# Blank padding rows of a sorted token buffer: written over whole regions in an early stage, or per expert right behind the routing

## The reference

```python
scores = softmax(x @ gate_w.T + gate_b)
dispatch = top-2 scores on their experts, 0 elsewhere
for i in range(E):                      # a later expert overwrites an earlier one
    wi = dispatch[:, i:i+1]
    h = relu((x_flat * wi) @ w1[i].T + b1[i])
    y = h @ w2[i].T + b2[i]
    out = where(wi > 0, y, out)
```

## Time and profile before

| | us |
|---|---|
| median of 3 runs | 1758.62 (1758.52 to 1768.12) |
| the profiled execution | 1758.52 |
| its span | 1756.7 |
| PE, DVE, ACT, POOL busy | 1543.0, 1314.9, 1269.7, 520.7 |

### The profile page before, as it was taken

How to read it: one execution, slowest core, us unless ns; L and a number is a source line. 1 busy time by engine, 2 the same in 40 slices (tenths; PEclk the granted TensorE clock), 3 DMA queues, 4 the chain that set the end, 5 groups by cost and what they waited for, 6 DMA issues and landing times. The chain is left out here.

```text
span 1756.7 us, 39269 instructions
## 1 busy us (share of the span) xinstructions
PE 1543.0 (88%) x13958; PEld 838.3 (48%) x13958; DVE 1314.9 (75%) x1924; ACT 1269.7 (72%) x2451; POOL 520.7 (30%) x741
## 2 busy tenths in 40 slices
PE   5999999999988999999999999988999855374297
PEld 4555555555543344343434434436777522123286
DVE  2777777777758999999999999936555438865475
ACT  2777777777753999899989998977888668403186
POOL 0222222222244110101110012117898504223466
PEclk8999999999995999999999999999999966686599
DMA  2121123232204010011001101005443200003120
GB/s 74 29 90 54 54 72 123 72 123 72 86 22 127 11 31 13 5 23 31 4 9 31 28 4 38 5 4 98 97 83 80 47 0 0 0 0 138 53 69 32
DMA packets 49386, 84.80 MB, mean 48 GB/s; under 512 B 19232, under 2 KB 25128, under 8 KB 48752
## 3 DMA queue, kind: packets, MB, share of 16 engines
q1 hardware_dynamic: 43888, 76.25, 16.4%
q0 software_dynamic: 5376, 6.96, 1.5%
HBM read 32.78 MB, written 23.92 MB: 32 GB/s over the span
## 5 line engine op out<-in xcount | busy, mean ns | idle before, releaser
L1049 ACT ACTIVATE m_probs<-m_ring 128x512 f32<-128x512 f32 x1024 | 542.8, 598 | 81.1 <-PE m_ring L965 65.5
L1128 DVE TENSOR_REDUCE m_half_max<-m_pairs 128x2 f32<-128x1024 f32 x512 | 588.1, 1212 | 14.6 <-PE m_pairs L948 14.2
L435 DVE TENSOR_REDUCE a_neg_max<-a_scores 128x1 f32<-128x1024 f32 x257 | 310.5, 1215 | 91.7 <-PE a_scores L362 91.6
L423 ACT ACTIVATE a_probs<-a_scores,a_neg_max 128x1024 f32<-128x1024 f32 x256 | 285.1, 1114 | 124.6 <-DVE a_neg_max L435 124.6
L980 PE MATMUL m_acc<-m_probs,m_v_aug 128*32 128x256 f32 (+1 forms) x4032 | 329.0, 399 | 0.0
L965 PE MATMUL m_ring<-m_q_max,m_k 32*128 32x512 f32 x1024 | 319.3, 501 | 3.9 <-DVE m_q_max L1142 3.0
L948 PE MATMUL m_pairs<-m_k,m_q 32*128 32x512 f32 x1024 | 265.2, 515 | 13.5 <-DVE m_half_max L1128 9.9
L362 PE MATMUL a_scores<-a_q,a_k_own 64*128 64x512 f32 x516 | 261.2, 623 | 6.5 <-ACT a_probs L423 5.6
L362 PE MATMUL a_scores<-a_q,a_k_other 64*128 64x512 f32 x516 | 259.5, 623 | 0.5
L965 PEld LDWEIGHTS m_ring<-m_q_max,m_k 32*128 32x128 f32 x1024 | 146.7, 184 | 219.0 <-ACT m_probs L1049 115.7
L471 POOL TENSOR_TENSOR a_scaled<-values,a_inv 128x128 f32<-128x128 f32 x256 | 102.0, 399 | 366.7 <-DVE a_inv L453 235.7
(11 more groups left out here) (279 smaller groups left out, 2087.0 us busy)
## 6 DMA issues: line engine op xcount, KB each, us to landing
sorted_tokens<-a_blank SPq DMA_DIRECT2D x8, 2176.0 KB
e_gates<-sorted_results SPq DMA_DIRECT2D x64, 256.0 KB, 8.5
a_k_other<-a_k_own SPq DMA_DIRECT2D x66, 128.0 KB, 2.3
m_k<-m_k_init SPq DMA_DIRECT2D x8, 512.0 KB, 7.0
m_q<-xT SPq DMA_DIRECT2D x8, 512.0 KB, 7.6
f_records<-sorted_tokens SPq DMA_DIRECT2D x40, 68.0 KB, 1.8
e_w<-e_w_dram SPq DMA_DIRECT2D x1, 2064.0 KB, 8.0
xT<-x_t_dram SPq DMA_DIRECT2D x1, 2048.0 KB, 7.7
```

Source lines behind the costliest of these rows:

```text
L423: nc.scalar.activation(probs[:, g, :], scores[:, slot(h * G + g), :], ACT.Exp, bias=neg_max[:, g:g + 1], accum_out=total[:, g:g + 1]).then ...
L435: nc.vector.tensor_reduce(neg_max[:, i % G:i % G + 1], scores[:, slot(i), :], AX, ALU.max, negate=True).then_inc(max_done, 1)
L1049: nc.scalar.activation(probs[:, u % SLOTS, head, :], ring[:, bank, :], ACT.Exp, scale=0.5).then_inc(ring_taken, 1)
L1128: nc.vector.tensor_reduce(half_max[:, pair // PAIRS % 2, at:at + 2], pairs[:, pair % 2, :, :], AX, ALU.max).then_inc(pair_taken, 1)
```

## The change

The blank records are no longer written in the first attention. There `blank`, its three semaphores, POOL's memset, `rows_of`, `fill` and the wait for `filled` are taken out, and the input `blank_rows` goes.

In the place stage there is a new tile `blank`, [128, 16, 136]. POOL sets it to zero at the start, waits for `order` and casts 16 columns of it (the `order` array grows by as many) into the row numbers. SP then waits for `blank_set`, behind its loads, and writes the 8 tiles at the end of `scratch` in one DMA (1024 records, 544 KB). DVE, when the last batch is placed, copies the 8 first free rows of the experts to `pad_at` and tells SP (`pads_known`). SP loads each into a register and writes 128 blank records there (68 KB), eight times. Only then does it go on to the table; and it waits for all nine writes (`padded_done`) beside the wait for the scatters.

```diff
@@ -222,8 +210,7 @@
 
-def first_attention_stage(core, xT, y, w_q, w_k, values, loads, scratch, blank_rows):
+def first_attention_stage(core, xT, y, w_q, w_k, values, loads):
 
@@ -263,10 +250,6 @@
         loaded = core.sem("a_loaded")
-        blank = core.sb("a_blank", [D, BLANK_ROWS, RECORD], F32, st)
-        blank_zero = core.sem("a_blank_zero")
-        blank_rows_in = core.sem("a_blank_rows_in")
-        filled = core.sem("a_filled")
         CREDIT = G
@@ -289,29 +272,6 @@
-                def rows_of(e):
-                    sp.wait_ge(blank_zero, 1)
-                    if e:
-                        sp.wait_ge(filled, 32 * e)
-                    sp.dma_start(blank[:, :, D:].bitcast(U32), blank_rows[:, e, :, :]).then_inc(blank_rows_in, 16)
-                def fill(e):
-                    sp.wait_ge(blank_rows_in, 16 * (e + 1))
-                    all_rows = blank[:, :, :].rearrange("p j d -> p (j d)")
-                    at = e * REGION
-                    if e == E:
-                        at += (SORT_TILES - UNUSED) * TILE
-                        sp.dma_start(scratch[at:at + UNUSED * TILE, :].rearrange("(p j) d -> p (j d)", j=BLANK_ROWS),
-                                     all_rows).then_inc(filled, 16)
-                        return
-                    wide = [D, N // (D * BLANK_ROWS), BLANK_ROWS * RECORD]
-                    sp.dma_start(scratch[at:at + N, :].rearrange("(c p j) d -> p c (j d)", p=D, j=BLANK_ROWS),
-                                 all_rows.unsqueeze(1).broadcast_to(wide)).then_inc(filled, 16)
-                    sp.dma_start(scratch[at + N:at + REGION, :].rearrange("(p j) d -> p (j d)", j=BLANK_ROWS),
-                                 all_rows[0:TILE // BLANK_ROWS, :]).then_inc(filled, 16)
 
@@ -319,14 +279,6 @@
                         sp.dma_start(to, at).then_inc(loaded, 16)
-                    else:
-                        e, at = divmod(head - len(loads), 2)
-                        if e <= E:
-                            if at == 0:
-                                rows_of(e)
-                            else:
-                                fill(e)
-                sp.wait_ge(filled, 16 * (2 * E + 1))
                 sp.wait_ge(keys_doubled, DUP * (TILES + 1))
@@ -457,7 +409,6 @@
             def _(pool):
-                nc.gpsimd.memset(blank[:, :, :], 0.0).then_inc(blank_zero, 1)
                 pool.wait_ge(zeroed, 1)
@@ -1878,9 +1829,18 @@
 
+SORT_TILES = (N + E * (TILE - 1)) // TILE + 1
+SORT_TILES += -SORT_TILES % 4
+TABLE = SORT_TILES + 2
 PER = BANK // D
 
+REGION = N + TILE
+UNUSED = 8
+RECORD = D + 8
+DUMP = E + UNUSED
+U32 = mybir.dt.uint32
+I32 = mybir.dt.int32
 
@@ -1902,8 +1862,8 @@
     at = D + E * (PER_BATCH + 1)
-    tile_rows, rows_of_out = order[:, at:at + TABLE], order[:, at + TABLE:at + TABLE + TILES]
-    at += TABLE + TILES
+    tile_rows, rows_of_out = order[:, at:at + TABLE], order[:, at + TABLE:at + TABLE + TILES + DUMP]
+    at += TABLE + TILES + DUMP
     region, earlier_first = order[:, at:at + E], order[:, at + E:at + 2 * E]
@@ -1912,6 +1872,8 @@
         eps = core.sb("p_eps", [D, 1], F32, st)
+        blank = core.sb("p_blank", [TILE, DUMP, RECORD], F32, st)
+        pad_at = core.sb("p_pad_at", [1, E], I32, st)
         turned = core.ps("p_turned", [TILE, 2, BANKS, BANK], st)
@@ -1953,7 +1915,11 @@
         recorded = core.sem("p_recorded")
+        blank_zero = core.sem("p_blank_zero")
+        blank_set = core.sem("p_blank_set")
+        pads_known = core.sem("p_pads_known")
         table_made = core.sem("p_table_made")
+        padded_done = core.sem("p_padded_done")
         scattered = core.sem("p_scattered")
@@ -1978,9 +1944,18 @@
                     sp.dma_start(to, at).then_inc(loaded, 16)
+                sp.wait_ge(blank_set, 1)
+                last = E * REGION + (SORT_TILES - UNUSED) * TILE
+                sp.dma_start(scratch[last:last + UNUSED * TILE, :].rearrange("(t p) d -> p t d", p=TILE),
+                             blank[:, E:, :]).then_inc(padded_done, 16)
+                sp.wait_ge(pads_known, 1)
+                for e in range(E):
+                    at = sp.value_load(pad_at[0:1, e:e + 1], min_val=0, max_val=E * REGION)
+                    sp.dma_start(scratch[ds(at, TILE), :], blank[:, e, :]).then_inc(padded_done, 16)
                 sp.wait_ge(table_made, 1)
                          for t in range(PER)]
+                sp.wait_ge(padded_done, 16 * (E + 1))
                 sp.wait_ge(scattered, 16 * TILES)
@@ -2137,6 +2112,8 @@
 
+                    then(nc.vector.tensor_copy(pad_at[0:1, :], start[0:1, :]))
+                    dve.sem_inc(pads_known, 1)
                     tt(count[:, :], start[:, :], region, ALU.subtract)
@@ -2163,7 +2140,7 @@
                 dve.wait_ge(order_in, 16)
-                nc.vector.tensor_copy(records[:, :, D + 1].bitcast(U32), rows_of_out).then_inc(recorded, 1)
+                nc.vector.tensor_copy(records[:, :, D + 1].bitcast(U32), rows_of_out[:, 0:TILES]).then_inc(recorded, 1)
                 then(nc.vector.tensor_copy(counts[:, :, 0], region))
@@ -2174,6 +2151,10 @@
             def _(pool):
+                nc.gpsimd.memset(blank[:, :, :], 0.0).then_inc(blank_zero, 1)
+                pool.wait_ge(blank_zero, 1)
+                pool.wait_ge(order_in, 16)
+                nc.gpsimd.tensor_copy(blank[:, :, D + 1].bitcast(U32), rows_of_out[:, TILES:]).then_inc(blank_set, 1)
                 for b in range(B):
@@ -2482,7 +2463,7 @@
                     constants.append((tiles.q[0][:, g, :].bitcast(F32), xT[:, PAD + N:PAD + N + S]))
-                first_attention_stage(core, xT, y, w_q, w_k, values, constants, scratch, a["blank_rows"])
+                first_attention_stage(core, xT, y, w_q, w_k, values, constants)
             tiles.add(core, st)
@@ -2602,15 +2583,9 @@
         np.broadcast_to(np.arange(TABLE) * TILE, (D, TABLE)),
-        row[:, None] + TILE * np.arange(TILES),
+        row[:, None] + TILE * np.arange(TILES + DUMP),
         np.broadcast_to(np.arange(E) * REGION, (D, E)),
-    behind_end = N + (row[:, None] * BLANK_ROWS + np.arange(BLANK_ROWS))
-    blank_rows = np.zeros((D, E + 1, BLANK_ROWS, RECORD - D), np.uint32)
-    for e in range(E):
-        blank_rows[:, e, :, 1] = N + TILE * e + (behind_end - N) % TILE
-    blank_rows[:, E, :, 1] = behind_end + TILE * E
 
@@ -2629,7 +2604,6 @@
         "s_w": np.ascontiguousarray(s_w.transpose(2, 0, 1)),
-        "blank_rows": blank_rows,
         "s_vecs": np.ascontiguousarray(s_vecs),
```

More of the change, by code:

```diff
@@ L25 @@
 E = 8
-SORT_TILES = (N + E * (TILE - 1)) // TILE + 1
-SORT_TILES += -SORT_TILES % 4
-TABLE = SORT_TILES + 2
-REGION = N + TILE
-UNUSED = 8
-RECORD = D + 8
-DUMP = E + UNUSED
-BLANK_ROWS = 8
-U32 = mybir.dt.uint32
-I32 = mybir.dt.int32
 class Core:
```

## The result

| | before | after |
|---|---|---|
| median us | 1760.0 (1756.97 to 1770.54, 20 runs) | 1772.05 (1762.65 to 1781.8, 20 runs) |
| ratio, 95% interval | | 1.0058 (1.0040 to 1.0078) |
| span of the profiled execution | 1756.7 | 1781.0 |

The change costs 12 us of the medians, by the interval 7 to 14 us. The profiled execution of after took 1783.15 us, above every other run of it, so its span isn't to be read whole. I followed the same DVE instructions through both traces: the distance after minus before moves by -1.0 us up to the first heads, then by +4.2 in the second attention, +6.3 and +6.0 around 1160 to 1235 us, +8.1 in the place stage and +0.7 behind it: 24.3 us.

What follows compares the result with a forecast made beforehand. POOL's scatters were taken as the path of the place stage. Profiled 1758.52 us + 0 + 0.5 + 0 + 0 + 0 = 1759.0, 1759.1 against the median, stated as 1759; range 1753 to 1766.

Steps and rivals of the forecast that it cites:

- 1. First attention: First attention: removing the small loads, fills and POOL's memset gains 0, at most 0.3 us.
- 2. Start of the place stage: Place stage start: POOL's memset runs beside DVE's first instructions and costs 0.5 us, range 0 to 2.0.
- 3. and 4.: Place stage: the tail write of 544 KB and DVE's extra copy ahead of the table each cost 0.
- 5.: Place stage, SP: eight register loads and pad writes at 1.16 us each end before the scatters land; cost 0.
- SP's pad chain becomes the path: Place stage: SP's pads, dearer beside scatters, outlast them; +4.5 us by issue, +6.6 by landing; chance 0.11.
- The rival of the stall: Place stage: DVE's third-batch stall goes (-5.55 us) or moves, a second in the fourth batch giving +6.3; chance 0.16.
- Fills cost something: First attention: the removed fills had cost time, so the kernel gains 0.3 us, giving 1758.8; chance 0.04.

Runs made afterwards that it cites:

- both: The kernel before, its first-attention fills kept, with the change's whole new part of the place stage added; ratio 1.0055 (1.0035 to 1.0075).
- the second profile of after: The changed kernel measured and profiled once more, nothing altered; ratio to before 1.0038 (1.0016 to 1.0061).
- the second profile of before: The kernel before measured and profiled once more as a control, nothing altered; ratio 0.9993 (0.9971 to 1.0015).
- act_queue: The changed kernel with the eight register loads and pad writes on ACT's queue instead of SP's; ratio to before 1.0033 (1.0009 to 1.0058).
- gap_each: The kernel before with 4 idle semaphore increments of POOL behind each scatter; ratio 1.0001 (0.9978 to 1.0023).
- shift64: The changed kernel with 64 idle semaphore increments of SP ahead of the pads; ratio to before 1.0072 (1.0051 to 1.0094).

## Why the prediction was wrong

It said 1759 us (1753 to 1766, within 1%); the median is 1772, within 1% by its ratio but outside the range. 1.4 us of the 13 us lie in the kernel before, whose median of 20 runs is 1760.0 for the 1758.6 of three. By its steps:

1. First attention: right, a gain of 0. The two heads that held a fill take the same with none (28.88 us; before), only the DMA share falls:

```profile
241.00:269.88 28.88, 28.12 (x354) 15.79 (x352) 21.04 (x35) 20.73 (x36) 6.37 (x17) 1.00 0.08 18
```

 POOL's memset gave nothing either. In the first profile of after DVE's memset starts at 22.60, for 23.24, but that is not the change's: the kernel both, which keeps POOL's memset, and the second profile of after, which has none, show 23.30 and 23.37.

```profile
22.60 2.62 DVE L390 MEMSET a_scaled<- 128x3072 f32 x1 [8.01 <-PEq L189]
```

```profile
22.59 1.00 POOL L460 MEMSET a_blank<- 128x1088 f32 x1 [22.12 <-POOLq L201]
23.30 2.62 DVE L438 MEMSET a_scaled<- 128x3072 f32 x1 [8.86 <-PEq L201]
```

```profile
23.37 2.62 DVE L390 MEMSET a_scaled<- 128x3072 f32 x1 [8.90 <-PEq L189]
```

 By the first heads both is 0.9 us ahead of the first profile of before, the second profile of before 0.7, and the two of after 1.0 and 0.8. So the 1.0 us that two expectations above count as a gain of the change is a difference between profiles.

2. Start of the place stage: the 0.5 us did not come. DVE's first instruction still takes 0.29 us beside the memset, and the first slot cast is 14.71 us behind the issue of `order`, before 14.70.

```profile
1601.89 1.91 POOL L2154 MEMSET p_blank<- 128x2176 f32 x1 [3.60 <-POOLq L1726]
1601.93 0.29 DVE L2136 TENSOR_TENSOR p_turn_w<-consts_sb 128x128 f32<-128x128 f32 x1 [0.32 <-PEq L1726]
```

3. and 4. The tail write went out at 1604.51 and nobody waited for it; DVE's copy cost nothing. Both right.

5. **This step failed**, and in one term: eight pads at 1.16 us. The row was right for the work and wrong for its surroundings; those 36 loads of the earlier trace rows run where POOL issues no scatter up to 1669.9 us and then, until they end at 1693.5, one every 1.8 us or more. The chain took 2.40 us a pad, above the 1.36 us at which the rival decides, ended at 1670.7, and the register loads ended at about 1673, 9.6 us behind the scatters for 1.5: +8.1 us. The rival "SP's pad chain becomes the path" had the mechanism and its place, at a chance of 0.11, and stopped at +4.5 us for the chain, 1.92 us a pad, since it priced only the DMA's issue dearer and not the five instructions ahead of it. The trace of before did hold it: the stall of the third batch, in which DVE "waits for nothing that the profile shows" and ACT too. I took it for a property of DVE's code that might move, and did not look at how far apart its single instructions start (0.70 or 1.4 us, over and over) or at what ran beside it, the ninth to the sixteenth scatter of the earlier trace rows. With that, a pad of six instructions could have been put at 4.2 us or more, at 0.70 us each, until 2.7 us behind the last scatter. That is hindsight: in before's second row, where the pads were to go, no step was that long.

 The rival of the stall: it neither went nor moved (17.47 us for 17.15). Fills cost something: no.

The loss of 1.0058 in the first comparison is 10 us, the stage 8.1 of them in the same profiles; 1.0038 in the second is 7 us, the stage 6.2. The rest is inside the intervals.

## What to carry to other kernels

When an engine's instructions stall with no releaser, look at their single starts and at what another engine does in those microseconds: a stall that belongs to a neighbour can fall on whatever the change puts beside that neighbour. A chain costed by a row from another stage needs the same neighbours there; here the slack was 1.6 us, and the chain ended 9.6 us later behind the cast than its row from the other stage had it. In this kernel writes whose addresses are known early (0.48 us each) went out beside a dense row of scatters at no cost; a chain of register loads did not, unless the scatters were broken up.

## What the runs showed of the hardware, unexpected

- Beside POOL's indirect DMAs that start 1.26 us apart, small instructions of DVE and SP come to start 0.70 us (or 1.4) apart, those of ACT in act_queue and of POOL itself in gap_each too. In rows without a gap it began between 9.2 and some 14 us into the row, and ended 2.5 to 3.4 us behind the row's last scatter (2.7 in before and in after). Gaps of 2.1 us between each eight scatters take all but a trace of it away. It isn't a backlog of transfers: the packets of each scatter in after are over within 1.3 us of the end of its issue.
- What lies behind it is open. It does not come in every row: before's four register loads, 13 us into the second row, go at nearly their usual pace (2.0 us between the first and the last, 1.7 in after behind the scatters), those of gap_each, 13 us into its own, take 5. A fetch of the next block of instructions does not fit shift64, in which no packet of the instruction queue stands beside SP's long steps. All executions here were recorded by the profiler, which has a record for each instruction; whether the recording has a part in the slow mode, no run shows. The spacing of scatters at which it begins wasn't measured.
- A memset of POOL beside a DVE subtraction of two SBUF operands changed nothing (0.29 us with it and without), and one beside a memset of DVE neither (2.62 us; the start moves between 22.2 and 24.0 us over the profiles, with POOL's memset or without).
